# Two node stages written out group by group, and the order by source read while relation rows are gathered: a four-block graph network on one core

## The reference

```
L0: mean of x[src] over dst, @ W_neigh.T + b
L1: sage1 -> sage2 -> gat (2 heads) ; rgcn (4 relations) ; fused = [h2, h_gat, h_rgcn] @ fusion_W + fusion_b, scaled to length 1
L2: h = [x[src], x[dst], edge_attr] @ W1 + b1 ; batch norm over the edges, relu ; @ W2 + b2
    sums = segment_sum(msgs, src) ; out = sums / (counts + 1) + x
L3: out = x @ W0 + segment_sum(h[edge_type, src] * edge_weight, dst), h = x @ W[r] for 8 relations ; / degree
```

## Time and profile before

| | us |
|---|---|
| median of 3 runs (10212.11 to 10216.0) | 10212.68 |
| profiled execution, its own time | 10201.99 |
| its span | 10199.8 |
| POOL busy | 6692.3 (66%) |
| PE busy | 6706.4 (66%) |
| DVE busy | 5144.5 (50%) |
| ACT busy | 1308.2 (13%) |

### The profile page before, as it was taken

How to read it: one execution, slowest core, us unless ns; L and a number is a source line. 1 busy time by engine, 2 the same in 40 slices (tenths; PEclk the granted TensorE clock), 3 DMA queues, 4 the chain that set the end, 5 groups by cost and what they waited for, 6 DMA issues and landing times. The chain is left out here.

```text
span 10199.8 us, 143982 instructions
## 1 busy us (share of the span) xinstructions
PE 6706.4 (66%) x31287; PEld 5127.7 (50%) x31287; DVE 5144.5 (50%) x16272; ACT 1308.2 (13%) x3084; POOL 6692.3 (66%) x7546
## 2 busy tenths in 40 slices
PE   2787755556677896705888746665566668866665
PEld 1666533334566654404777524444455557733343
DVE  6555655554455534665777434444222226644445
ACT  0000000000000015700000100001122225530000
POOL 1777647777777777767777777773577750027775
PEclk8666655556666685557999955556677779975555
DMA  1222112222333330004777512222566663332222
GB/s 53 52 52 52 45 49 50 51 51 62 98 104 104 104 106 17 2 10 138 220 219 220 169 35 52 52 52 55 146 187 184 185 148 106 100 121 52 52 52 53
DMA packets 556744, 932.76 MB, mean 91 GB/s; under 512 B 161514, under 2 KB 336326, under 8 KB 556302
## 3 DMA queue, kind: packets, MB, share of 16 engines
q0 software_dynamic: 271264, 606.93, 22.5%
q1 hardware_dynamic: 279038, 299.48, 9.4%
q10 hardware_dynamic: 6384, 25.69, 0.6%
HBM read 788.54 MB, written 143.03 MB: 91 GB/s over the span
## 5 line engine op out<-in xcount | busy, mean ns | idle before, releaser
L728 PE MATMUL sage_window<-sage_hot,sage_message 128*128 128x128 f32 x4992 | 1450.2, 433 | 751.7 <-DMA sage_message<-t_x,sage_index_stage 307.2
L728 PEld LDWEIGHTS sage_window<-sage_hot,sage_message 128*128 128x128 f32 x4992 | 1087.5, 297 | 1114.5 <-issue 615.6
L728 PE MATMUL block_window<-block_hot,block_message 128*128 128x128 f32 x3328 | 1186.8, 457 | 672.6 <-DMA block_message<-t_rel,block_index_stage 345.3
L728 PEld LDWEIGHTS block_window<-block_hot,block_message 128*128 128x128 f32 x3328 | 787.3, 294 | 1047.3 <-issue 657.5
L668 DVE TENSOR_TENSOR first_acc<-first_acc,sage_window 128x128 f32 (+1 forms) x1664 | 590.9, 355 | 874.2 <-PE sage_window L728 867.7
L1871 POOL DMA_INDIRECT eh_message<-t_q,eh_stage x880 | 832.2, 946 | 251.9 <-issue 233.9
L578 POOL DMA_INDIRECT sage_message<-t_x,sage_index_stage x832 | 817.4, 982 | 237.6 <-issue 222.1
L728 PE MATMUL gat_window<-gat_hot,gat_message 128*128 128x128 f32 x6656 | 848.0, 281 | 187.7 <-DVE gat_hot L586 96.8
L578 POOL DMA_INDIRECT gat_message<-t_h,gat_index_stage x832 | 793.6, 954 | 237.5 <-issue 222.1
L578 POOL DMA_INDIRECT sage_message<-t_s,sage_index_stage x832 | 788.9, 948 | 237.5 <-issue 222.1
L578 POOL DMA_INDIRECT rgcn_message<-t_rel,rgcn_index_stage x832 | 788.8, 948 | 237.5 <-issue 222.1
(11 more groups left out here) (474 smaller groups left out, 11121.3 us busy)
## 6 DMA issues: line engine op xcount, KB each, us to landing
eh_window<-t_p SPq DMA_DIRECT2D x880, 64.0 KB
t_hidden<-eh_hidden SPq DMA_DIRECT2D x110, 512.0 KB
sc_rows<-t_hidden SPq DMA_DIRECT2D x110, 512.0 KB, 3.6
eh_low_rows<-t_low SPq DMA_DIRECT2D x110, 256.0 KB, 3.5
t_rel<-n_h ACTq DMA_DIRECT2D x7, 3584.0 KB
eh_message<-t_q,eh_stage POOLq DMA_INDIRECT x880
block_message<-in_x,block_index_stage POOLq DMA_INDIRECT x832, 2.5
sage_message<-t_x,sage_index_stage POOLq DMA_INDIRECT x832, 2.5
```

The source lines that it names most:

```text
L728: last = nc.tensor.matmul(ps[k][:, b, :], message[u][:, f:f + P], hot[:, u, j * P:(j + 1) * P], start=(j == 0), stop=(j == heads - 1))
```

## The change

The order by source moves into the rgcn aggregation: a class `SourceOrder` loads a block of 128 edge tiles of `t_rec` twice (once by tile, once by edge, the latter in pieces of 16 bytes), and after every seventh turn DVE picks and splits one block; SP stores the parts. The block search and the split of W1 move into after_gat. Both `load_weights` blocks go; SP loads the weights during the aggregation and at the end of the scatter. after_rgcn and after_block2 lose their loops: the groups are written out, with two buffers for most tiles, and PE, ACT and DVE get new orders. In after_rgcn the squares go from DVE to ACT, the input copies and the copy of x go, and POOL issues the stores. In after_block2 SP stores the rows one node tile at a time. `source_order` and `edge_weights` go. The old bodies stand above; the core of the diff:

```diff
@@ aggregate
+        if orders:
+            @block.sync
+            def _(sp):
+                for b in range(2):
+                    order.load(sp, b)
+                for b in range(EB):
+                    order.store(sp, b)
+                    if b + 2 < EB:
+                        order.load(sp, b + 2)
+                order.finish(sp)
...
-            if own or fuses:
+            if orders:
+                for b in range(EB):
+                    with dve.Fori(b * NT // EB, (b + 1) * NT // EB, 1) as it:
+                        turn(it, True)
+                    order.split(nc, dve, b)
+                with dve.Fori(NT, ITERS, 1) as it:
+                    turn(it, False)
+            elif own or fuses:
                 with dve.Fori(0, NT, 1) as it:
                     turn(it, True)
                 with dve.Fori(NT, ITERS, 1) as it:
@@ after_gat
+            sp.dma_start(rest[:], a["L2_gnn_W1"][2 * C:2 * C + 2, :]).then_inc(rest_in, 16)
...
+            sp.wait_ge(parted, 3)
+            for n, (_, of_weight) in enumerate(PAIRS):
+                sp.dma_start(m.t_w1c[2 * n:2 * n + 2, :], parts[:, of_weight]).then_inc(parts_kept, 16)
+            sp.wait_ge(parts_kept, 16 * len(PAIRS))
...
+            link = chain(dve, m)
+            for b in range(EB):
+                link(nc.vector.tensor_scalar(tile[:, b:b + 1], m.column[:], float(b * P), None, ALU.add))
+                link(nc.vector.tensor_scalar(ended[:, b], m.block_end[:, 0:NT], tile[:, b:b + 1], 0.0, ALU.is_le, ALU.add,
+                                             accum_out=m.block_of[:, b:b + 1]))
+            link(nc.vector.tensor_scalar(m.block_of[:], m.block_of[:], float(NT - 1), None, ALU.min))
+            nc.vector.tensor_scalar(base[:], m.block_of[:], float(P), None, ALU.mult).then_inc(block_found, 1)
             for g in range(NG):
...
+            dve.wait_ge(block_turned, EB)
+            link(nc.vector.tensor_copy(m.block_base[:], row[:, 0:TP]))
+            dve.wait_ge(rest_in, 16)
+            split_in_three(nc, dve, link, rest[:], part[:], [parts[:, n] for n in range(3)], parted)
...
+            pe.wait_ge(block_found, 1)
+            for b in range(EB):
+                nc.tensor.transpose(row[:, b * P:(b + 1) * P], base[:, b:b + 1], m.ident[:]).then_inc(block_turned, 1)
@@ after_rgcn
+            for g in range(NG):
+                if g >= 2:
+                    sp.wait_ge(fused, g - 1)
+                sp.dma_start(f[:, g % 2], rows_of(m.t_f, g, C)).then_inc(loaded[g % 2], 16)
+
+        @block.gpsimd
+        def _(pool):
+            for g in range(NG):
+                pool.wait_ge(pq_taken, g + 1)
+                pool.dma_start(rows_of(m.t_p, g, C), pq[:, :, 0:C]).then_inc(stored, 16)
+                pool.dma_start(rows_of(m.t_q, g, C), pq[:, :, C:2 * C]).then_inc(stored, 16)
+            pool.wait_ge(stored, 32 * NG)
...
+            def lengths(g):
+                act.wait_ge(fused, g + 1)
+                for j in range(GN):
+                    nc.scalar.activation(square[:, j, :], out[:, g % 2, j, :], ACT.Square, accum_out=length[:, g % 2, 0, j:j + 1]).then_inc(squared, 1)
+                act.wait_ge(squared, (g + 1) * GN)
+                nc.scalar.activation(length[:, g % 2, 1], length[:, g % 2, 0], ACT.Sqrt).then_inc(length_root, 1)
+
+            def keep(g):
                 act.wait_ge(turned, g + 1)
+                if g >= 2:
+                    act.wait_ge(pq_made, g - 1)
+                nc.scalar.copy(x_t[:, g % 2], ps_t[:, 0:GN, :]).then_inc(kept, 1)
 
             def take(g):
                 act.wait_ge(pq_made, g + 1)
+                if g >= 1:
+                    act.wait_ge(stored, 32 * g)
                 nc.scalar.copy(pq[:], ps[:, 0:GN, :]).then_inc(pq_taken, 1)
 
+            lengths(0)
+            for g in range(NG):
+                if g + 1 < NG:
+                    lengths(g + 1)
+                b.square_root(act, g)
+                keep(g)
+                if g >= 1:
+                    take(g - 1)
             take(NG - 1)
...
+            def join(g):
+                dve.wait_ge(loaded[g % 2], 16 * (g // 2 + 1))
                 dve.wait_ge(made, g + 1)
+                if g >= 2:
+                    dve.wait_ge(b.norm_ready, (g - 1) * GN)
+                nc.vector.tensor_tensor(out[:, g % 2], ps_f[:, 0:GN, :], f[:, g % 2], ALU.add).then_inc(fused, 1)
+
+            def add(g):
                 dve.wait_ge(length_root, g + 1)
+                nc.vector.tensor_scalar(length[:, g % 2, 1], length[:, g % 2, 1], 1e-12, None, ALU.max).then_inc(capped, 1)
+                dve.wait_ge(capped, g + 1)
+                nc.vector.reciprocal(length[:, g % 2, 2], length[:, g % 2, 1]).then_inc(inverted, 1)
+                dve.wait_ge(inverted, g + 1)
                 for j in range(GN):
+                    nc.vector.scalar_tensor_tensor(out[:, g % 2, j, :], out[:, g % 2, j, :], length[:, g % 2, 2, j:j + 1], m.x[:, g * GN + j, :],
                                                    ALU.mult, ALU.add).then_inc(joined, 1)
                 dve.wait_ge(joined, (g + 1) * GN)
+                b.figures(dve, g, out[:, g % 2])
+
+            join(0)
+            for g in range(NG):
+                if g + 1 < NG:
+                    join(g + 1)
+                add(g)
+                b.apply(dve, g, out[:, g % 2], m.x[:, tiles_of(g), :])
...
             def products(g):
                 pe.wait_ge(kept, g + 1)
+                if g >= 1:
+                    pe.wait_ge(pq_taken, g)
...
 
             fuse(0)
+            for g in range(NG):
+                if g + 1 < NG:
+                    fuse(g + 1)
+                turn(g)
+                if g >= 1:
+                    products(g - 1)
             products(NG - 1)
@@ scatter_by_source
+            for tile, source in loads:
+                sp.dma_start(tile, source).then_inc(weights_in, 16)
+            sp.wait_ge(weights_in, 16 * len(loads))
@@ after_block2
+            for g in range(NG):
+                if g >= 1:
+                    dve.wait_ge(b.norm_ready, g * GN)
                 for j in range(GN):
...
+                nc.vector.tensor_tensor(y[:], y[:], m.x[:, tiles_of(g), :], ALU.add).then_inc(summed, 1)
+                dve.wait_ge(summed, g + 1)
+                b.figures(dve, g, y)
+                b.apply(dve, g, y, m.x[:, tiles_of(g), :])
...
             def take(g, banks):
                 for n in banks:
                     act.wait_ge(h_made, g * BANKS + n + 1)
+                    if g >= 1 and n % 2 == 0:
+                        act.wait_ge(stored[n // 2], 16 * g)
+                    nc.scalar.copy(h[:, n // 2, (n % 2) * 4 * C:(n % 2 + 1) * 4 * C], ps_h[:, (g * BANKS + n) % 4, :]).then_inc(h_taken, 1)
+
+            def keep(g):
+                act.wait_ge(turned, g + 1)
+                if g >= 2:
+                    act.wait_ge(h_made, (g - 1) * BANKS)
+                    act.wait_ge(root_made, g - 1)
+                nc.scalar.copy(x_t[:, g % 2], ps_t[:].rearrange("p j n -> p (j n)")[:, 0:GW]).then_inc(kept, 1)
...
+            b.square_root(act, 0)
+            keep(0)
+            take_root(0)
+            for g in range(NG):
+                if g + 1 < NG:
+                    b.square_root(act, g + 1)
                 take(g, range(EARLY))
+                if g + 1 < NG:
+                    keep(g + 1)
                 take(g, range(EARLY, BANKS))
+                if g + 1 < NG:
+                    take_root(g + 1)
...
+            def messages(g, banks):
+                for n in banks:
+                    if g * BANKS + n >= 4:
+                        pe.wait_ge(h_taken, g * BANKS + n - 3)
+                    nc.tensor.matmul(ps_h[:, (g * BANKS + n) % 4, :], x_t[:, g % 2, (n // 2) * P:(n // 2 + 1) * P],
+                                     w.w8[:, (n % 2) * 4:(n % 2) * 4 + 4].rearrange("p r n -> p (r n)"), start=True, stop=True).then_inc(h_made, 1)
+
+            turn(0)
+            root(0)
+            for g in range(NG):
+                messages(g, range(EARLY))
+                if g + 1 < NG:
+                    turn(g + 1)
+                messages(g, range(EARLY, BANKS))
+                if g + 1 < NG:
+                    root(g + 1)
+
+        @block.sync
+        def _(sp):
+            for g in range(NG):
+                for j in range(GN):
+                    n = g * GN + j
+                    sp.wait_ge(h_taken, g * BANKS + 2 * j + 2)
+                    sp.dma_start(m.t_rel8[n * P:(n + 1) * P, :], h[:, j, :]).then_inc(stored[j], 16)
+            for j in range(GN):
+                sp.wait_ge(stored[j], 16 * NG)
@@ SourceOrder (new)
+    def load(self, sp, b):
+        records = self.m.t_rec[b * P * P:(b + 1) * P * P, :]
+        if b >= 2:
+            sp.wait_ge(self.picked[b % 2], 4 * (b // 2))
+        sp.dma_start(self.by_tile[:, b % 2], records.rearrange("(t p) k -> t p k", p=P)).then_inc(self.loaded[b % 2], 16)
```

(74 more changed lines are left out.)

299 lines of the change are left out of this document (110 added, 189 removed).

## The result

| us | before | changed |
|---|---|---|
| median of 4 runs | 10213.83 (10212.11 to 10216.0) | 10144.68 (10140.95 to 10149.1) |
| profiled execution, its own time | 10201.99 | 10140.95 |
| its span | 10199.8 | 10139.1 |

Changed over before is 0.9932, 95% interval 0.9915 to 0.995: 0.7% faster. The predicted 10155 is 10 too high, and the time lies inside the range of 10100 to 10190.

The account below looks back on a forecast made before the run. POOL's gathers were taken to bound rgcn, and serial chains after_rgcn and the stages behind it. −45.3 + 3 + 33 − 49 = −58 on the median of 10212.68 gave 10155 us, range 10100 to 10190.

Parts of the forecast that it names:

- Part 1: source_order and edge_weights go as stages: −45.3 us, their work in after_gat hidden beside POOL's record scatters at +0.
- Part 2: Seven splits of about 4 us on DVE and the loads by edge inside rgcn: +3 us, bounds 0 and +17.
- the slower rival: In rgcn, 16-byte loads outlast seven turns and POOL stops; gain lost at about 155 us a load, +117 at 170; chance .05.
- the cover: In rgcn, ACT stages a half 7.35 us before POOL takes it, so a 4 us stop of DVE fits: +0.
- a possible stop for the whole of a split: In rgcn, all 4 us of a copying split could stop POOL's descriptor writing: +28 us.
- Part 3: after_rgcn in its new order, products at 1.2 GHz taking 13.1 us: 211 us against 177.9, +33.
- The sign that I gave for the stage: after_rgcn 205 to 216 us, seven products of 13 us at clock 0.50, PE standing some 8 us before each turn.
- the four periods: after_rgcn's middle: four periods of 29.0 us from fuse, handover, DVE, turn and products, 116 us.
- the head to the third fuse's end: after_rgcn from entry to the end of its third fuse: 28.5 us.
- the tail: after_rgcn from the next-to-last norm through last products, store and exit: 64.8 us, +2 for POOL issuing the last stores.
- Rival B: after_rgcn's products get the full clock: −11 us there, −102 in all, 10110; chance .22.
- Part 4: after_block2 without weights block and store wait, PE dense for 93.5 us: −49 us, range −40 to −51.

Follow-up runs that it names:

- the long splits: Changed kernel with 32 more dependent copies of 256 columns in each split; rgcn 1263.9 us against 1239.6, repeated 1289.6 against 1271.5.

## Why the prediction was right

**Part 1** held: the stage's 45.3 us went and nothing came back. Undone, it gives +46.0. Its work in after_gat is hidden: the scatters have 145.7 + 50.0, before 145.3 + 50.0.

**Part 2** held. Splits of 3.5 to 3.8 us (4 foretold), rgcn +1.5 (+3), of which nothing stands clear of what executions differ by. The load is 14 us, inside my 5 to 34; the slower rival needed 155. The DMA share beside the loads was wrong: 1.32 where I had at most .5, without harm. I gave the cover as ACT's 7.35 alone; it is 9 to 11 where it was measured. The Trainium skill, "SBUF — State Buffer", on DVE blocking DMA, has POOL shut out of descriptor writing while a fast copy runs. I had taken from that a possible stop for the whole of a split. So taken, the long splits would have stopped POOL for most of 10.5 us each. Their 32 copies are .33 us each, and the gathers beside them took up to 1.01 in place of .95: the traces show some 5% and no stop (the longest single gather, once, is 1.39).

**Part 3** had the mechanism right and its size off, +24.5 for +33. Products took 13.0 (13.1 foretold) at 0.50. The sign that I gave for the stage, 205 to 216 us, was missed: it took 202.4. The terms that were mis-sized are fuse above all, then the pause. I took 14 × .39 = 5.5 for a fuse, but rows of .39 overlap and start .22 apart: at full clock a fuse is 3.3 to 3.4, and behind the products, its first part at half clock, 4.8 to 5.1. The pause is 8.10, for .25 + 8.4, and the turn 1.55 to the next start, for 1.75. So the four periods are 110.1 (27.5 each) for 116, the head to the third fuse's end 25.7 for 28.5, and the tail 66.7 for 66.8. From the last taking to the next stage it is 8.25 us in place of 5.84, so POOL's stores cost 2.4 in the tail, for my 2.

Rival B, products at the full clock, did not come. Its reason did show in the experiments: the clock is up when the pause is closed, and rises in time when the one-row matmuls are gone. The Trainium skill, "TensorE: Matmul & The Clock Gate", Part 1, says that activity releases the throttle and that idling brings it back. The second half the traces bear out (pauses of 8.10 and 4.31 us, and of 1.00 behind products, then half clock); of the first they show that dense work is not enough: with a one-row matmul behind each full one 13 us pass at 1.2 GHz, without them the granted clock is 1.00 after 3.1 at the latest. Why the one-row matmuls keep it down is not shown.

**Part 4** held, −52.7 for −49, with two errors that nearly cancel. PE's dense part took 98.1 (8929.96 to 9028.0) for 93.5: a root term takes 1.5, where I put .5 against a row of 1.77 in before. (Six turns and root terms are also 8.6 by my own figures and not 9.2.) The end went the other way: block3's staging is 3.4 behind the last copy, where I had 4 for the last store and 7 of edges that I could not place.

On the median the gain is 69 and on the profiled executions 61; the prediction went by the latter, and the difference is what executions differ by. That the 61 is so near the foretold 58 is luck: against the forecast the three stages came out 14 better (8.5 in after_rgcn, 3.7 in after_block2, 1.5 in rgcn), and the changed kernel's profiled execution lost 11 to that of before in code that is the same in both.

## What to carry to other kernels

Where a wait for another engine stands in PE's order, put the work that is ready ahead of it, not behind: it costs no buffer here, fills the pause, and where no pause is left keeps the clock, 81 us for a few moved lines. Check with the granted clock what a stretch of matmuls will run at, since an order that lengthens PE's pauses is paid twice. Price a bias that is added by a one-row matmul: at the full clock it was 4.0 of 7.3 us here. Store per tile as soon as a tile is whole: seven stores of 0.52 MB for a group hid but for the last, where one of 3.67 MB for each group cost 63 us in all.

## What I had not expected of the hardware

With one-row matmuls between full ones TensorE stayed at a granted clock of 0.50 through 13.0 us of dense work; without them the clock was up within 3.1 us and the same products took 4.3 to 4.7. Behind products with them a pause of 1.00 us was enough for the clock to fall. On two of the chips the aggregation loops ran a fifth longer, the kernel before as a whole 12574 and 12737, with code written out straight at its usual pace; POOL's gathers still took .95 each, it was DVE and PE that stood. What holds them there is open.
